# k with q, pairs of u and halves of f1 as 64-row matmuls among the attention scores, three piece banks, and a new order

## What is computed

```python
xn = layernorm(x)                                 # 8 batches, 1024 tokens, 256 features
u, v, q, k = split(silu(xn @ W1 + b1), 4)         # 256 each, 16 heads of 16
scores = einsum('bqhd,bkhd->bhqk', q, k)
attn = silu(scores) / 1024
av = einsum('bhqk,bkhd->bqhd', attn, v)
attention = layernorm(av * u, gamma, beta) @ W2 + b2
h = layernorm(xn, ln1) @ ternary(w1).T + b1       # 1024 hidden features
h = layernorm(gelu(h), ln2) @ ternary(w2).T + b2
out = x + attention + h
```

## Time and profile before

| what | value |
|---|---|
| median of 3 runs | 1492.8 us (1492.14 to 1492.99) |
| profiled execution | 1493.36 us |
| its span, first to last instruction | 1491.6 us |
| mean granted TensorE clock | 0.997 |
| busy: PE, weight loads, DVE, ACT, POOL | 98%, 53%, 60%, 81%, 7% |
| chain that ended last: PE, DVE, ACT | 88%, 5%, 4% |
| HBM read, written | 79.84 MB, 41.94 MB |

### The profile page before, as it was taken

How to read it: one execution, slowest core, us unless ns; L and a number is a source line. 1 busy time by engine, 2 the same in 40 slices (tenths; PEclk the granted TensorE clock), 3 DMA queues, 4 the chain that set the end, 5 groups by cost and what they waited for, 6 DMA issues and landing times.

```text
span 1491.6 us, 25963 instructions
## 1 busy us (share of the span) xinstructions
PE 1464.8 (98%) x9942; PEld 784.7 (53%) x9942; DVE 895.3 (60%) x1719; ACT 1208.9 (81%) x1273; POOL 97.4 (7%) x197
## 2 busy tenths in 40 slices
PE   8999999999999999999999999999999999999998
PEld 7445555455554555554554455545555455554544
DVE  5557655576546854468654685447755476545745
ACT  4788888888788887887878878788788887888885
POOL 2001000010000100001000010000100001000001
PEclk9999999999999999999999999999999999999999
DMA  7351052410524106340153402443033510435100
GB/s 248 81 128 57 15 132 65 130 57 15 156 71 100 58 15 156 95 104 29 30 155 99 113 1 59 126 129 84 1 89 110 142 57 5 115 81 142 29 1 29
DMA packets 67996, 123.49 MB, mean 83 GB/s; under 512 B 12832, under 2 KB 14496, under 8 KB 66976
## 3 DMA queue, kind: packets, MB, share of 16 engines
q1 hardware_dynamic: 67712, 121.57, 29.9%
q10 hardware_dynamic: 160, 0.26, 0.1%
HBM read 79.84 MB, written 41.94 MB: 82 GB/s over the span
## 4 chain that ended last, share of the span: by engine, by line
PE 88%; DVE 5%; ACT 4%; issue 1%; DVEq 1%; DMA 0%; ACTq 0%
PE outs L1101 30%; PE scores L1079 22%; PE fill L1136 10%; PE fill L1170 9%; PE fill L1154 7%; PE fill L1186 3%; PE fill L1163 3%; ACT attn L636 3%; PE fill L1145 2%; DVE tmp L917 1%; PE fill L1126 1%; DVE hid L900 1%; ACT hid L681 1%; DVE st L813 1%; ACT L636 1%
## 5 line engine op out<-in xcount | busy, mean ns | idle before, releaser
L636 ACT ACTIVATE attn<-scores 128x1024 f32<-128x1024 f32 x1024 | 991.4, 1023 | 225.3 <-PE scores L1079 220.6
L1101 PE MATMUL outs<-attn,V 128*32 128x512 f32 x4096 | 494.3, 600 | 0.0
L1079 PE MATMUL scores<-QS,KS 64*128 64x512 f32 x2048 | 387.7, 452 | 8.3 <-ACT attn L636 7.0
L1079 PEld LDWEIGHTS scores<-QS,KS 64*128 64x128 f32 x2048 | 163.0, 184 | 300.4 <-ACT attn L636 241.5
L1101 PEld LDWEIGHTS outs<-attn,V 128*32 128x32 f32 x4096 | 107.2, 109 | 235.8 <-issue 235.1
L900 DVE SCALAR_TENSOR_TENSOR hid<-fill,ratq,fb1b 128x512 f32<-128x512 f32 x128 | 96.1, 751 | 77.6 <-PE fill L1154 72.3
L917 DVE TENSOR_TENSOR tmp<-fill,l2g 128x512 f32<-128x512 f32 x128 | 88.6, 692 | 88.6 <-PE fill L1163 81.1
L1170 PE MATMUL fill<-Wq,hgh 128*128 128x256 f32 x504 | 128.2, 292 | 2.0 <-DVE hgl L924 1.1
L1136 PE MATMUL fill<-xp,W1h 128*128 128x512 f32 x384 | 128.4, 416 | 0.5 <-DVE xp L949 0.5
L1170 PE MATMUL fill<-Wq,hgl 128*128 128x256 f32 x504 | 123.1, 282 | 0.0
L1170 PEld LDWEIGHTS fill<-Wq,hgh 128*128 128x128 f32 x504 | 95.8, 190 | 18.9 <-issue 14.6
(11 more groups left out here) (138 smaller groups left out, 1349.3 us busy)
## 6 DMA issues: line engine op xcount, KB each, us to landing
QS<-q_scratch SPq DMA_DIRECT2D x254, 128.0 KB, 3.3
k_scratch<-kst SPq DMA_DIRECT2D x64, 256.0 KB
q_scratch<-qst SPq DMA_DIRECT2D x64, 256.0 KB
KS<-k_scratch SPq DMA_DIRECT2D x128, 128.0 KB, 3.2
KS<-k_scratch SPq DMA_DIRECT2D x256, 64.0 KB, 3.4
out_dram<-part SPq DMA_DIRECT2D x15, 512.0 KB, 2.6
xin<-in_x SPq DMA_DIRECT2D x7, 1024.0 KB, 5.1
xin<-in_x SPq DMA_DIRECT2D x2, 512.0 KB, 4.3
```

Source lines behind the costliest of these rows:

```text
L636: nc.scalar.activation(attn_of(g)[:, 2 * hf:2 * hf + 2, :], SP[:, 2 * hf:2 * hf + 2, :], ACT.Silu).then_inc(s_silu, 1)
L1079: ins = mm(SP[:, j, :], KS[rows, pair, t * P:(t + 1) * P], QS[rows, pair - c * PPC, h * HALF:(h + 1) * HALF], start=True, stop=True)
L1101: ins = mm(OP[32 * j:32 * j + 32, g // RUN % 2, :], V[:, t, c * HPC // 2 + j, o * DH:o * DH + 2 * DH], attn_of(g)[:, n, :], start=(o == 0 ...
```

## The change

It does the following.

- A round begins one group later: PE issues the products with v, the scores of group 2n + 1, the pieces, and the scores of group 2n + 2 at the end of the round.
- k with q, u of both feature halves, and the two halves of one f1 tile become groups in halves (`PARTNERS`). Where a round holds such a group (at most one per round), it stands directly behind the odd scores. Each contraction over 128 rows is cut into two of 64 rows: in phase 0 piece A runs on the upper 64 rows and piece B on the lower ones, in phase 1 the other way round, in two banks. The first half of the next group's scores stands between the phases, the second half behind. Phase 1 waits for the end of phase 0 (`s_half`), as both add to the same banks.
- Further f1 pieces in the round follow behind as full-array pieces, as do f2 and g. The functions for g and f2 in halves are there, but nothing is grouped for them (`GROUPED`).
- ACT does the silu of the odd group, the steps ahead of the group in halves, the first half of the next group's silu, the other steps, and the second half. In rounds without a group all steps stand ahead of both halves.
- OP has one bank, FP three; the set-up's sums go to FP's third bank. Each run of 16 groups waits for DVE's output of the run before.
- The tables are new; `EARLIER` is gone. kq.0.1 stands in round 30, vs.0 in round 29, gelu.3 in round 24, px in round 8, all u and kq of c = 1 in rounds 6 to 9.

The diff, cut to its core:

```diff
-EARLIER = {1: parsed("k.1.0")}
+PARTNERS = {"kq": lambda c, h: (("k", c, h), ("q", c, h)), "u": lambda h: (("u", 0, h), ("u", 1, h)),
+            "f1": lambda t: (("f1", t, 0), ("f1", t, 1)), "g": lambda t: (("g", t, 0), ("g", t, 1))}
...
+def pieces_of(b, n):
+    pieces = [xs for xs in steps_of(b, n) if xs[1][0] in FILLERS]
+    first = next((i for i, (x, s) in enumerate(pieces) if s[0] in GROUPED), len(pieces))
+    size = 0 if first == len(pieces) else 1 if pieces[first][1][0] == "f2" else 2
+    return pieces[:first], pieces[first:first + size], pieces[first + size:]
...
+GROUPED = ("k", "u", "f1")
+FILLS = 3
...
-        OP = ctx.enter_context(nc.psum_tensor("outs", [P, 2, HALF], F32))
-        FP = ctx.enter_context(nc.psum_tensor("fill", [P, 2, HALF], F32))
+        OP = ctx.enter_context(nc.psum_tensor("outs", [P, HALF], F32))
+        FP = ctx.enter_context(nc.psum_tensor("fill", [P, FILLS, HALF], F32))
...
             def body(b):
                 for n in range(ROUNDS):
-                    for g in (2 * n, 2 * n + 1):
-                        silu_group(b, g)
...
-                    for x, s in steps_of(b, n):
+                    nb, ng = next_group(b, 2 * n + 1)
+                    for hf in range(2):
+                        silu_half(b, 2 * n + 1, hf)
+                    steps = list(steps_of(b, n))
+                    group = pieces_of(b, n)[1]
+                    behind = steps.index(group[0]) if group else len(steps)
+                    for x, s in steps[:behind]:
                         step(x, *s)
+                    if nb < NB:
+                        silu_half(nb, ng, 0)
+                    for x, s in steps[behind:]:
+                        step(x, *s)
+                    if nb < NB:
+                        silu_half(nb, ng, 1)
...
-                if g % RUN == 0 and (b or g >= 2 * RUN):
-                    pe.wait_ge(s_z, DC * NH * b + g // RUN - 1)
+                if g % RUN == 0 and (b or g):
+                    pe.wait_ge(s_z, DC * NH * b + g // RUN)
...
+            def crossed(steps, phase):
+                if phase == 0:
+                    for x, step in steps:
+                        wait_free(x, step)
+                        wait_data(x, step)
+                else:
+                    pe.wait_ge(s_half, CROSSED.index(steps[0]) + 1)
+                count = 4 if steps[0][1][0] == "f1" else 6
+                for n in range(count):
+                    for half in range(2):
+                        x, step = steps[half ^ phase]
...
+                        rows = slice(half * P // 2, (half + 1) * P // 2)
...
+                            ins = mm(FP[:, k, :].rearrange("p (i n) -> p i n", i=2), w[rows, kc, col:col + P],
+                                     xp[rows, 2 * h:2 * h + 2, part, kc, :],
+                                     start=phase == 0 and n == 0, stop=phase == 1 and n == count - 1)
...
+                if phase == 0:
+                    ins.then_inc(s_half, 1)
...
             def body(b):
                 for n in range(ROUNDS):
-                    scores(b, 2 * n)
...
-                    scores(b, 2 * n + 1)
-                    for x, s in steps_of(b, n):
-                        step(x, *s)
...
+                    if group:
+                        for x, s in lead:
+                            step(x, *s)
+                    for hf in range(2):
+                        scores(b, 2 * n + 1, hf)
...
+                    if not group:
+                        for x, s in lead:
+                            step(x, *s)
...
+                    for hf in range(2):
+                        if group:
+                            in_halves(group, hf)
+                        if nb < NB:
+                            scores(nb, ng, hf)
...
+                    for x, s in full:
+                        if group:
+                            step(x, *s)
```

More of the change, by code:

```diff
@@ L107 @@
+    "y.1",
+    "kq.1.1",
+    "f1.0",
+    "",
+    "f1.1",
+    "",
+    "y.3 gelu.0 f1.2 f1.3",
+    "f1.4",
+    "ln2.0 nrm2.0 f1.5",
+    "",
+    "",
+    "g.0",
+    "f1.6 f2.0 f1.7 gelu.1",
+    "gelu.2 g.1",
+    "",
+    "ln2.1 nrm2.1",
+    "f2.1",
+    "",
+    "ln1 xn.0 g.2 ln2.2",
+    "",
+    "",
+    "xt.0",
+    "",
+    "f2.2 xn.1",
+    "g.3 nrm2.2",
+    "",
     "xt.1",
-    "xn.2 f2.4 xt.2",
-    "",
-    "k.0.0",
-    "g.5.0",
-    "g.5.1 gelu.3 v.0 xn.3 v.1",
+    "f2.3",
@@ L138 @@
 LAST_ROUNDS = {
[L139 to L150, removed]
+    16: "ln2.1 nrm2.1",
+    17: "f2.1",
+    18: "g.2 ln2.2",
+    19: "",
+    20: "f2.2",
+    21: "g.3 nrm2.2",
+    22: "f2.3",
+    23: "g.4",
+    24: "f2.4 gelu.3 g.5 ln2.3",
+    25: "nrm2.3 f2.5 zs.0 zt.0 zt.1",
@@ L370, in hybrid_block_kernel @@
         s_mv3, s_rs3 = sem("z_moments"), sem("z_rstd")
-        s_fill = [sem("filled0"), sem("filled1")]
-        s_evac = [sem("evacuated0"), sem("evacuated1")]
+        s_fill = [sem(f"filled{k}") for k in range(FILLS)]
+        s_evac = [sem(f"evacuated{k}") for k in range(FILLS)]
+        s_half = sem("first_halves_done")
         s_xh = sem("x_high_part")
@@ new lines, in summed @@
+            def summed(steps, phase):
+                (x, step), = steps
+                t = step[1]
+                if phase == 0:
+                    wait_free(x, step)
+                pe.wait_ge(s_hg, 2 * T * x + 2 * t + 2)
+                for n in range(4):
+                    for w in (hgh, hgl):
+                        for half, (k, turn) in enumerate(BANKS[x, step]):
+                            rows = slice(half * P // 2, (half + 1) * P // 2)
+                            ins = mm(FP[:, k, 0:D], w[rows, phase, n * P:(n + 1) * P], Wq2[rows, 4 * phase + n, :],
+                                     start=phase == 0 and n == 0 and w is hgh, stop=phase == 1 and n == 3 and w is hgl)
+                            if phase == 1 and n == 3 and w is hgl:
+                                ins.then_inc(s_fill[k], 1)
@@ L1280, in _ @@
                 step(0, *s)
+            for hf in range(2):
+                scores(0, 0, hf)
             for b in range(NB):
                 body(b)
-            pe.wait_ge(s_z, DC * NH * (NB - 1) + 3)
+            wait_evacuated(pe, *last_piece(2))
             last_hidden(0)
```

301 lines of the change are left out of this document (186 added, 115 removed).

## The result

The changed kernel takes **1510.65 us** (median of 4 runs, 1509.12 to 1511.65) against 1492.65 us for the kernel before: ratio 1.012, 95% interval 1.0102 to 1.0138, so 18 us slower. I had forecast 1500.5 us, slower by 7.7. The direction was right and the time lies in the wide range of 1487 to 1516, but it is outside the forecast's own 1494 to 1508, and more than half of the 18 us is not in my sum.

What follows compares the result with a forecast made beforehand. PE, busy 98% of the span, was taken as the bound, with a 4.81 us silu loop under short rounds. Middle blocks −3.7 + 2.0 + 2.7 = +1.0, six +6.0, block 0 +1.3, last +0.4: +7.7, 1500.5 us, range 1494 to 1508 (wide 1487 to 1516).

Steps and rivals of the forecast that it cites:

- what a slot costs: In groups in halves, a pair of 64-row matmuls was taken as 0.231 us, between 0.215 and 0.255.
- what the halves save: Per middle block, fewer changes of shape save 3.7 us, while waits and bare loads inside the groups add 2.0.
- The term of 0.20: In groups followed by a full-array piece, one change of shape goes, saving 0.20 us; 3 such groups in a middle block.
- what order and banks cost in the middle blocks: Per middle block, floor rounds, gelu delays, vs.0 and bank waits come to 7.6 us against 4.9 before, +2.7.
- The floor of 4.81 us: The loop of scores, two silus, scores, outs sets 4.81 us under every round whose pieces take less than 1.44.
- gelu.3's round: gelu.3 with its table switches holds ACT 4.53 us: a round of 7.58, next scores 1.3 late; some 9 us expected in the trace.
- Sum +7.7 on the profiled execution's 1493.36: Whole kernel: six middle blocks +6.0, block 0 +1.3, last block +0.4, giving 1501.1 us, or 1500.5 as median.
- The last block, without xt and v, +0.4: In the last block, which lacks the xt and v pieces, the change was to cost 0.4 us.
- One outs bank costs nothing: DVE's output must be done a whole round later, and PE reaches it three us after outs ended: no cost.
- late k rows: Rival: k rows land late at block starts, two us in seven blocks, 1515 us; 6%.
- slots neither cheap nor dear: Two rivals: cheap slots at 0.215 us, giving 1486.5 us, 10%; dear slots bound by issue at 0.255, giving 1521, 10%.
- gelu's lateness not absorbed: Rival: the 1.8 us delay per block of gelu.3 and vs.0 vanishes into floor rounds behind them, 1488 us; 13%.

Runs made afterwards that it cites:

- e1: The changed kernel with no group in halves, so its new order and three banks with every piece whole: 1520.21 us, ratio 1.018 to the kernel before.
- e5: The changed kernel with extra products without use in the empty round 16 and the last block's round 25: 1504.36 us, ratio 1.0078 to the kernel before.
- e3: The changed kernel's code and three banks with the order of the kernel before, halves only where partners already stand together: 1485.41 us, ratio 0.9949.
- e6: The changed kernel with f2.1 moved from round 17 back into round 16, leaving round 17 empty: 1513.98 us, ratio 1.0139 to the kernel before.
- e13: e3 with the statistics ln2.1 moved to round 16 behind outs, f1.7 as a pair in round 17, g.2.0 in round 18: 1485.72 us, ratio 0.995.
- e15: e3 with ln2.1 moved to round 16 behind outs, and otherwise only f1.7.0 put ahead of g.2.0 in round 17: 1478.73 us, ratio 0.9904.

## Why the prediction was wrong

**Right: what a slot costs.** 0.228 us, taken as 0.231 (bounds 0.215 and 0.255); the first slot of the second phase bares 0.11, taken as 0.07. By the Trainium skill (TensorE: Matmul & The Clock Gate, Part 3, The mechanism) every load in the same rows should have lain bare, hidden by nothing. The six slots of the first phase above show none bare. Changes of shape (rows and columns of the array), counted in the two traces from 33 us on, fell from 1023 to 852; forecast was 1020 to 849.

**Nearly right: what the halves save.** -3.7 + 2.0 = -1.7 a block, measured -1.2 (e1 against the changed kernel). My terms come to 0.29 for a group of u with u alone in its round, 0.17 for k with q and 0.18 for f1; the rounds of block 3 give 0.28 and 0.17, then 0.23 to 0.28, then 0.06 to 0.17. The term of 0.20 for the groups with a full-array tail is wrong: they lose 0.08 to 0.14 each.

**Right: what order and banks cost in the middle blocks, at full clock.** I had +2.7. Measured: banks -0.55 (181.15 to 180.6), order +3.0 (180.6 to 183.6), together +2.5. The floor of 4.81 us, the empty round 16 (4.97) and gelu.3 (1.2, taken as 1.3) are all there. But gelu.3's round lasts 8.1 us and not "some 9": only a part of the delay falls in it, the rest in the next round. Blocks 1 to 3 last 182.45 us, worked out as 182.3.

**Wrong: "Sum +7.7 on the profiled execution's 1493.36".** Every term of that sum is a duration read at full clock, and no term asks what PE's new standing still does to the clock. I had written "round 16 with no piece, 4.81 − 3.37 = 1.44" and priced it as idle time only. It costs 1.7 us more in each of blocks 4 to 6, and the wait behind gelu.3 2.7 in the last block: 7.9 of the 10.5 us missing. That the falls come from these waits is shown by e5, where only the idle places were filled. The granted clock of 0.997 stood in the table of the kernel before, and I took it as given.

**Wrong: "The last block, without xt and v, +0.4".** It is +5.0: 2.7 clock, which leaves 2.3 for the order and the halves. With xt and v gone, rounds 24, 25, 28 and 29 take 8.10 + 6.85 + 6.11 + 6.16 = 27.2 us (round 25 from e5, at full clock) for 23.6 in the kernel before; e1, with whole pieces, has the same 6.1 in rounds 28 and 29. The rest of the error is here (1.9) and in the middle blocks (7.4 for 6.0 without the clock, taking e5's blocks), less 0.5 at the start and 0.1 in block 0.

**Right for this order only: "One outs bank costs nothing".** In the changed kernel outs waits 0.0 us. In the old order it waits 8.1 (e3). My reason, that PE reaches DVE's output a whole round later, leaves out what else DVE has to do by then. The step held because the new order has ln2.1 in round 16, behind the output, and not because that round is empty: in e6, with f2.1 in round 16, outs waits 0.0 as well, and so it does in e13 to e15, where the old order has ln2.1 there.

**The rivals.** PE waited for a DMA once, 0.2 us, so no late k rows; slots neither cheap nor dear; gelu's lateness not absorbed. Most of the 10.5 us missing came from a mechanism that had no rival of its own. That the time still lies between 1487 and 1516 is luck: that width was there for other mechanisms.

## What to carry to other kernels

Before giving work a cheaper form, look at what sets the length of the stretch it stands in: a product in a round that lasts its four silus is free already, and putting two together so that they can share the array costs a full round's excess (1.0 us here) to save at most 0.3. When a change opens waits on TensorE, price them twice, as idle time and as the risk of half clock behind them; an extra product in the gap is a cheap test and can be a cure. When a kernel loses a buffer, look in the trace for what the engine that empties it does just before.

## What the runs showed of the chip that I had not expected

- **Short waits can be enough for the clock to fall.** In round 16 no single wait is longer than 0.42 us, PE is at work for 3.8 of 4.97 us, and 97% of the whole span; yet the clock went from 2.4 to 1.2 GHz behind it in three of eight blocks of the profiled execution. The Trainium skill (TensorE: Matmul & The Clock Gate, Part 1, A second HAM failure mode) describes such short idling, in a kernel that cycles through PSUM banks, as a cause of swings between the two levels. This trace agrees, with waits of 0.35 to 0.42 us for ACT. What decides between the blocks with equal instructions I did not try to settle.
- **Work without use can save time.** Three products of 512 columns in a round of 4.97 us left it at 4.96 and kept the clock.
- **What half clock costs.** In blocks 4 to 6 it cost 1.7 us each time, most of it in one set of outs (3.62 us for 1.92). In the last block the clock was 0.64 over a round of 9.6 us, which cost 2.7.
